# Routed tokens gathered in quarter rows and turned by VectorE instead of TensorE, in a fused MetaFormer block with a mixture of experts

## What is computed

```python
x = x + conv_ref(ln_c(x), ...)            # per channel and image a gate from mean, std, max and a median
t = to_tokens(x)                          # 2048 tokens x 512 channels
h = ln_t(t)                               # normalized tokens
logits = h @ router_w.T                   # 8 experts, the best one is taken
e, w = top_1(logits), sigmoid(top_value)
t = t + w * (silu(h @ w1[e]) * (h @ v1[e])) @ w2[e]      # routed expert
t = t + (silu(h @ sg) * (h @ su)) @ sd                   # shared expert
```

## Time and profile before

| | |
|---|---|
| three runs | 413.93 us median, 413.44 to 414.0 |
| span of the profiled execution, first to last instruction | 411.6 us |
| median less span | 2.3 us, what lies around the instructions |
| TensorE matmuls busy | 94% of the span |
| VectorE / ScalarE / GpSimd busy | 63% / 39% / 33% |

### The profile page before, as it was taken

The page is one execution under the profiler, slowest core; times in us unless marked ns, Lnnn a source line. Parts: engine busy times, 40 slices in busy tenths (PEclk is TensorE's granted clock), DMA queues, the critical chain, the costliest instruction groups (busy, mean ns, idle before and its releaser), DMA issues.

```text
span 411.6 us, 6789 instructions
## 1 busy us (share of the span) xinstructions
PE 385.1 (94%) x1982; PEld 303.8 (74%) x1986; DVE 258.2 (63%) x475; ACT 161.2 (39%) x274; POOL 134.6 (33%) x186
## 2 busy tenths in 40 slices
PE   5875659999999999999999999999999999999994
PEld 2442238888888788887888888888888888888883
DVE  6997876555857865656875557547375744676322
ACT  3996852223344324211116245153254515354110
POOL 7787811000100100005030245425535442446201
PEclk9998999999999999999999999999999999999999
DMA  8900502011201561140041469726546773752210
GB/s 321 397 2 0 204 1 78 27 51 60 90 30 53 187 247 53 53 153 27 32 133 41 128 217 323 282 98 256 204 134 219 294 258 118 262 182 71 86 37 30
DMA packets 14763, 55.96 MB, mean 136 GB/s; under 512 B 2575, under 2 KB 2575, under 8 KB 11280
## 3 DMA queue, kind: packets, MB, share of 16 engines
q1 hardware_dynamic: 9936, 40.93, 28.0%
q0 software_dynamic: 4800, 14.69, 10.0%
HBM read 43.02 MB, written 13.63 MB: 138 GB/s over the span
## 4 chain that ended last, share of the span: by engine, by line
PE 81%; DVE 7%; ACT 5%; issue 3%; POOL 2%; DMA 1%; DVEq 0%; POOLq 0%; ACTq 0%
PE GU L1255 47%; PE yb L1255 22%; PE th L1247 4%; PE tx L1240 4%; ACT tiles L534 2%; PE th L1284 2%; DVE search_junk L806 1%; ACT scratch L545 1%; ACT scratch L549 1%; DMA x_sb<-x_tok 1%; PE mb L1255 1%; DVE x_sb L864 1%; DVE tiles L862 1%; DVE bn_parts L871 1%; PE mb L1233 0%
## 5 line engine op out<-in xcount | busy, mean ns | idle before, releaser
L1255 PE MATMUL GU<-w_parts,xT 128*128 (+1 forms) x864 | 213.6, 395 | 0.0
L1255 PEld LDWEIGHTS GU<-w_parts,xT 128*128 128x128 f32 x864 | 158.3, 188 | 31.4
L1255 PE MATMUL yb<-w_parts,hT 128*128 (+1 forms) x420 | 102.6, 392 | 0.0
L1255 PEld LDWEIGHTS yb<-w_parts,hT 128*128 128x128 f32 x420 | 77.8, 188 | 15.7
L605 ACT ACTIVATE hT<-th 128x512 fp32r<-128x512 f32 x36 | 21.6, 599 | 170.8 <-PE th L1247 170.8
L472 POOL DMA_INDIRECT out<-x_sb,scatidx x20 | 37.6, 1879 | 92.5 <-DVE x_sb L1098 85.6
L922 DVE TENSOR_TENSOR w_parts<-w_raw,w_parts 128x2048 f32 (+1 forms) x24 | 54.9, 2288 | 7.4 <-issue 7.2
L907 DVE TENSOR_TENSOR hidden<-hidden,GU 128x512 f32<-128x512 f32 x36 | 24.8, 688 | 40.2 <-PE GU L1255 40.1
L522 ACT ACTIVATE w_parts<-w_raw 128x2048 f32 (+1 forms) x24 | 45.2, 1910 | 4.2 <-issue 3.9
L446 POOL TENSOR_TENSOR x_rstd<-x_mv,eps 128x1 f32<-128x1 f32 x16 | 3.0, 190 | 113.4 <-DVE x_mv L874 113.4
L901 DVE TENSOR_TENSOR hT<-th,hT 128x512 fp32r<-128x512 f32 x36 | 24.8, 689 | 23.9 <-ACT hT L605 23.6
(11 more groups left out here) (233 smaller groups left out, 339.8 us busy)
## 6 DMA issues: line engine op xcount, KB each, us to landing
w_raw<-weights SPq DMA_DIRECT2D x27, 1024.0 KB, 5.3
x_sb<-x_tok SPq DMA_DIRECT2D x8, 512.0 KB, 6.5
xn_d<-tiles SPq DMA_DIRECT2D x16, 256.0 KB, 2.0
z_d<-x_sb SPq DMA_DIRECT2D x16, 256.0 KB, 2.0
tiles<-xn_d,tokidx POOLq DMA_INDIRECT x20, 4.7
x_sb<-z_d,tokidx POOLq DMA_INDIRECT x20, 5.5
out<-x_sb,scatidx POOLq DMA_INDIRECT x20, 6.8
conv<-conv_par SPq DMA_DIRECT2D x1, 10.0 KB, 9.0
```

The costliest lines, as they stand in the source:

```text
L1255: last = pe.matmul(dst, left[:, lp, kc, :], wset(q, k, wp, kc), start=(i == 0), stop=(i == 3 * KC - 1))
```

## The change

Normalized rows are written with their channels interleaved: place 4c + f of a row holds channel 128f + c. TensorE's transposes of the shared stage read them back through the same view, with a step of four elements. A routed block is no longer gathered by one DMA of 128 rows of 512 floats, but by four DMAs of 128 rows of 128 floats (a quarter row each). The partition p of DMA j takes quarter p // 32 of the token in slot 32j + p % 32. VectorE then turns the buffer in one instruction of 32 x 32 transposes, which gives channels in the partitions (`turn_x`, into the SBUF tile `turned`, a part of `search_junk`). ScalarE and VectorE take the high and low parts from there (`turned_hi`, `turned_lo`), and TensorE's four transposes a block are gone. The indices of the quarter rows come from four small matmuls with a 0/1 matrix `dealer` (`deal_slots`) and one VectorE instruction (`quad_rows`).

```diff
+        turned = search_junk[:, 2 * P:2 * P + C]
+        dealer = turned.rearrange("p (j q r) -> p j q r", j=QUADS, q=QUADS)
...
+            xn_quads = xn_d.rearrange("t (q c) -> (t q) c", q=QUADS)
...
-                pool.indirect_dma_start(xg[:, b % RING, :], None, xn_d[:, :], rows(tokidx, b)).then_inc(xg_in[b % RING], 16)
+                for j in range(QUADS):
+                    pool.indirect_dma_start(xg[:, b % RING, j * P:(j + 1) * P], None, xn_quads, rows(quadidx[:, j, :], b)).then_inc(xg_in[b % RING], 16)
...
+            pool.wait_ge(quads_ready, 1)
             for b in range(RING):
                 gather_x(b)
...
-                pool.wait_ge(tx_done, NT + b - RING + 1)
+                pool.wait_ge(x_turned, b - RING + 1)
                 gather_x(b)
...
-                dve.tensor_scalar(tiles[:, u, :], tile_of(x_sb, t), x1_mv[:, u, 0:1], x1_rstd[:, u:u + 1], ALU.subtract, ALU.mult).then_inc(xn_ready, 1)
+                dve.tensor_scalar(interleaved(tiles[:, u, :]), tile_of(x_sb, t).rearrange("p (f c) -> p f c", f=KC),
+                                  x1_mv[:, u, 0:1], x1_rstd[:, u:u + 1], ALU.subtract, ALU.mult).then_inc(xn_ready, 1)
+
+            def turn_x(b, u, count):
+
+                dve.wait_ge(xg_in[u], count)
+                dve.wait_ge(xlo, b + NT)
+                dve.transpose(out=turned.rearrange("p (f j r) -> p f j r", f=KC, j=QUADS),
+                              in_=xg[:, u, :].rearrange("p (j c f) -> p f j c", j=QUADS, f=KC)).then_inc(x_turned, 1)
+
+            def turned_lo(n, slot):
+                dve.wait_ge(xhi, n + 1)
+                dve.wait_ge(x_turned, n - (NT - 1))
+                dve.tensor_tensor(xT[:, slot, LO, :, :], turned.rearrange("p (k t) -> p k t", k=KC),
+                                  xT[:, slot, HI, :, :].bitcast(F32), ALU.subtract).then_inc(xlo, 1)
...
+                if n == DEALER_AFTER:
+                    note(dve.tensor_copy(dealer, ident[:, :].rearrange("p (j r) -> p j r", j=QUADS).unsqueeze(2).to_broadcast([P, QUADS, QUADS, QROWS])))
...
+            def quad_rows():
+
+                dve.wait_ge(slots_dealt, 1)
+                dve.tensor_scalar(quadidx[:, :, :], tx[:, 0:QUADS * NB].rearrange("p (j b) -> p j b", j=QUADS), float(QUADS), quad[:, 0:1],
+                                  ALU.mult, ALU.add).then_inc(quads_ready, 1)
...
             def step(b, u, j, base):
+                ahead = (u + 2) % RING
+                turn_x(b + 2, ahead, j * (16 * QUADS) + 16 * QUADS * (base + 1 + (u + 2) // RING))
                 h_lo(b + NT, u % 2)
-                x_lo(b + (NT + 2), u % 2)
+                turned_lo(b + (NT + 2), u % 2)
                 gated(b + (NT + 1), 1 - u % 2)
...
-                    last = pe.transpose(tx[:, k * P:(k + 1) * P], src[:, k * P:(k + 1) * P], ident[:, :])
+                    last = pe.transpose(tx[:, k * P:(k + 1) * P], interleaved(src)[:, k, :], ident[:, :])
...
+            def deal_slots():
+
+                pe.wait_ge(slots_ready, 1)
+                for j in range(QUADS):
+                    last = pe.matmul(tx[:, j * NB:(j + 1) * NB],
+                                     turned[:, j * P:(j + 1) * P],
+                                     slotinfo[:, 0, 0:NB], start=True, stop=True)
+                last.then_inc(slots_dealt, 1)
...
-                pe.wait_ge(xg_in[ahead], j * 16 + 16 * (base + 1 + (u + 2) // RING))
-                transpose_x(n + 2, xg[:, ahead, :])
```

More of the change, by code:

```diff
@@ L24 @@
 RING = 4
+QUADS, QROWS = 4, 32
+DEALER_AFTER = 7
 SEARCH_FROM, SEARCH_TO = -24.0, 24.0
@@ L130, in program @@
         scatidx = sb("scatidx", [P, NB], U32)
+        quadidx = sb("quadidx", [P, QUADS, NB], U32)
+        quad_i = sb("quad_i", [P, 1], I32)
+        quad = sb("quad", [P, 1])
         rtmp = tiles[:, :, :].rearrange("p a c -> p (a c)")
@@ L226, in program @@
         slots_ready = sem("slots_ready")
+        slots_dealt = sem("slots_dealt")
+        quads_ready = sem("quads_ready")
+        x_turned = sem("x_turned")
         tables = sem("tables")
@@ L267, in spread_rows, with interleaved @@
             return scratch[:, of * P:to * P].rearrange("p (s b r) -> p s b r", s=to - of, b=B)
+        def interleaved(row):
+            return row.rearrange("p (c f) -> p f c", f=KC)
         def tile_of(buf, t):
@@ L595, in x_hi, with turned_hi @@
                 act.activation(xT[:, slot, HI, :, :], tx[:, :].rearrange("p (k t) -> p k t", k=KC), ACT.Copy).then_inc(xhi, 1)
+            def turned_hi(n, slot):
+                act.wait_ge(x_turned, n - (NT - 1))
+                act.activation(xT[:, slot, HI, :, :], turned.rearrange("p (k t) -> p k t", k=KC), ACT.Copy).then_inc(xhi, 1)
             def silu_gate(n, parity):
@@ L655, in _ @@
                     keep_logits(t)
-            x_hi(NT, 0)
+            turned_hi(NT, 0)
             for k in (GATE, UP):
@@ L661, in _ @@
             h_hi(NT - 1, 1)
-            x_hi(NT + 1, 1)
+            turned_hi(NT + 1, 1)
             silu_gate(NT, 0)
@@ L676, in step @@
                 h_hi(b + NT, u % 2)
-                x_hi(b + (NT + 2), u % 2)
+                turned_hi(b + (NT + 2), u % 2)
                 silu_gate(b + (NT + 1), 1 - u % 2)
@@ L713, in _ @@
             own(dve.tensor_copy(iota_f[:, :], iota_i[:, :]))
+            own(dve.tensor_scalar(quad_i[:, :], pidx_i[:, 0:1], QROWS.bit_length() - 1, None, ALU.logical_shift_right))
+            own(dve.tensor_copy(quad[:, :], quad_i[:, :]))
             own(dve.tensor_copy(pidx[:, :], pidx_i[:, :]))
@@ L1114, in _ @@
             h_lo(n + 2, 1)
+            quad_rows()
             block_experts()
@@ L1120, in _ @@
             gated(n + 4, 1)
-            x_lo(NT, 0)
+            turn_x(0, 0, 16 * QUADS)
+            turned_lo(NT, 0)
             add_shared(n + 3)
             lo_of(GATE, 1)
+            turn_x(1, 1, 16 * QUADS)
             h_lo(n + 4, 1)
-            x_lo(NT + 1, 1)
+            turned_lo(NT + 1, 1)
             gated(NT, 0)
@@ L1307, in _ @@
                 for k in (2 * half, 2 * half + 1):
-                    last = pe.transpose((th, tx)[half][:, k * P:(k + 1) * P], tiles[:, 0, k * P:(k + 1) * P], ident[:, :])
+                    last = pe.transpose((th, tx)[half][:, k * P:(k + 1) * P], interleaved(tiles[:, 0, :])[:, k, :], ident[:, :])
                 last.then_inc(tx_half if half == 0 else tx_done, 1)
@@ L1375, in _ @@
             transpose_h(n + 2, 1)
+            deal_slots()
             up_product(n + 3, 2, 0, 0, 0)
@@ L1380, in _ @@
             up_product(n + 4, 3, 1, 0, 0)
-            pe.wait_ge(xg_in[0], 16)
-            transpose_x(NT, xg[:, 0, :])
             down_product(n + 3, 0, 0, 0)
@@ L1385, in _ @@
             transpose_h(n + 4, 1)
-            pe.wait_ge(xg_in[1], 16)
-            transpose_x(NT + 1, xg[:, 1, :])
             up_product(NT, 0, 0, 1, 3)
@@ L1392, in step @@
                 n = b + NT
-                ahead = (u + 2) % RING
                 at, after = table_entries(pe, b, range(SET_COL, SET2_COL + 1))
```

## The result

The changed kernel takes 417.66 us in the median of four runs (417.46 to 417.95), the one before 413.9 us beside it (413.44 to 414.0). The ratio is 1.0094, 95% interval 1.0079 to 1.0108: slower by 3.8 us, where +1.9 was forecast. Differences of 0.2% can be told apart here, so the sign is certain.

A forecast was written before the change was run, and what follows sets the result against it. The prediction took TensorE as the bound, busy for all of the routed window. Its terms, -8.8 transposes, +1.1 dealing, +0.3 normalizing and +9.3 late gathers, made +1.9 us: 415.8 us, range 406.2 to 420.5.

The forecast's parts named there:

- strided transposes: Shared stage, TensorE reading with a step of four: taken as no cost, bounds nothing to 5.8 us.
- cover of VectorE's list: Routed steps behind gate-up steps: 0.1 us of slack left before h_lo; if gone, 2.5 us of stalls.
- rival D: Routed stage: VectorE becomes the bound, 18 turns adding 12 us; no chance of its own, price of 2.5 us in C.
- Transposes removed: Twenty routed blocks lose four TensorE transposes each: 8.8 us gained, a step falling from 9.09 to 8.65 us.
- Dealing: Before the routed stage, four index matmuls and a wait for tokidx on TensorE's path: 1.1 us lost, matmuls 0.6.
- Normalizing and the shared transposes: Shared stage: norm_tile's interleaved write delays the first tile, 0.3 us lost; the strided reads add nothing.
- The turn: Routed stage, VectorE's transposing instruction ahead of h_lo: 0.68 us each, bounds 0.55 to 1.22, barely covered.
- GpSimd's list: Routed stage: quarter gathers held by weight splits deliver x late, 145 us for 15 blocks, TensorE stalls 9.3 us; chance 0.55.
- the signs named: Profile rows expected if right: GpSimd nearly never idle, gathers of 2 to 3 us, turns awaiting x, down products awaiting h_lo.
- C: Rival: the 16-byte step costs double everywhere, 2.9 us in transposes, 2.5 behind gate-up steps; alone 411.9 us, chance 0.08.
- The net of the routed stage: Routed stage: gain of the removed transposes against stalls from late gathers, -8.8 and +9.3 us, forecast +0.5.
- C with A: Rival: doubled cost of the 16-byte step together with GpSimd being late, 418.7 us, chance 0.10.

The follow-up runs named there:

- runs: Changed kernel with no step of 16 bytes: tiles hold runs of 32 neighbouring channels, gate, up and router matrix rows laid out to match; 414.94 us, ratio 1.0027.
- no_hold_short: Changed kernel, routed weight splits read a PSUM bank in place of the high part, and the turn moves only 128 of 512 elements; 410.34 us, ratio 0.9911.
- one_gather: Changed kernel with each block of x gathered by one DMA instead of four, the turn kept; 416.1 us, ratio 1.0056.
- one_gather_short: Changed kernel with one gather DMA a block and a turn of only 128 of 512 elements; 411.14 us, ratio 0.9925.
- turn_late: Changed kernel with VectorE's turn placed behind h_lo, same work; 418.15 us, ratio 1.0110.
- no_hold: Changed kernel, the routed loop's weight splits read a PSUM bank in place of the high part in SBUF; 415.56 us, ratio 1.0032.
- short_turn: Changed kernel with the turn moving only 128 of 512 elements of a partition, all else kept; 416.73 us, ratio 1.0061.
- mixed2: As runs, but only two blocks in four quartered and turned, others gathered whole and transposed by TensorE, dealing behind the up product; 412.96 us, ratio 0.9972.
- turn_plain: Changed kernel with the turn reading runs of 32 neighbouring elements instead of every fourth one; 416.9 us, ratio 1.0071.
- turn_psum: Changed kernel with the turn writing to a PSUM bank instead of SBUF, both parts taken from there; 420.98 us, ratio 1.0172.
- no_deal: Changed kernel without the dealing matmuls, quad_rows taking indices from slotinfo; 419.45 us, ratio 1.0134.

## Why the prediction was right and wrong

The measured loss is twice the forecast one. For the number, the step that failed is the sum's term for the shared stage, above all the strided transposes, put at nothing; the 0.3 us that it had for both were 1.15 us. For the mechanism, it is the length of the turn and with it the cover of VectorE's list: rival D, taken for nothing by itself, is one of the two causes.

**Transposes removed, -8.8 us.** Right: 8.64 us a step.

**Dealing, 1.1 us.** 1.42 us. The four fp32 matmuls run as eight and take 0.91 us, the upper bound, where I took 0.6.

**Normalizing and the shared transposes, 0.3 us together.** The step that failed first. `norm_tile` took 0.744 us, inside its bounds, but the transposes, at "I take nothing, as no row shows an engine slowed by a layout", cost 0.035 us a tile (a row of four takes 0.39 us, before 0.355), 0.56 us in all, and a tile normalized late held TensorE for 0.39 us at 143.69. With 0.2 us at the first tile that makes 1.15 us, the 1.2 us between runs and no_hold_short. The rest of the 1.85 us is the fall of the clock (0.47) and the late first `norm_tile` (0.38), less the 0.14 us by which the execution was ahead; the prediction had no term for either. "No row shows it" was an argument for the middle of the bounds, not for their lower end.

**The turn, 0.68 us.** Mis-sized: 1.09 us, of which 0.39 is the step of 16 bytes. My two ends were 0.55 and 1.22 us, and I called the cover 0.1 us wide. With the turn at 1.09 it is gone. Rival D got no chance of its own and a price of 2.5 us. With GpSimd's list short, a turn of 1.09 us in place of 0.40 costs 5.0 us (one_gather less one_gather_short). That it is so much fits turn_late's rows, where the turn also heads the chain over ScalarE's high parts to the next split, which the slack of one step doesn't show.

**GpSimd's list, +9.3 us.** The length was right: 144.9 us for 145. Nineteen DMAs in that stretch were held by splits and lost 29.7 us (28 reckoned), three by `turned_lo` and lost 0.8 (2.6 reckoned). The hold is shown, and stalls of 8.4 us came for the 9.3 forecast. But they weren't the stalls I described: taken away alone the holds give 2.1 us (no_hold), and 6.4 us once the turn is short (short_turn to no_hold_short). "Unhindered, the turn of x(19) would have to start at 382.5" held for a TensorE that nothing else delays, and VectorE delayed it. The turn of x(19) did start at 392.55, for the 392 forecast, and the down product behind it started at 395.10 without an idle row: by then TensorE was as late as GpSimd. That the two times agree is in part luck: the list started at 240.9, not 237.7, and the landing was 2.7 us in the median, not the 5.7 I took:

```profile
DMA to landing us min/median/max: 2.4/2.7/6.9
```

So of the signs named, GpSimd without idle time, gathers of 2 to 3 us and waits of down products for `h_lo` came; so did a turn over 1 us, a sign of C, while the pitch of the shared transposes was 0.39/4 = 0.098 us, under its 0.11. The turns waited for x three times only, 3.7 us.

**The sum.** Between the two profiled executions 1.55 us too little are ahead of `fill_slots` and 0.3 the dealing; of the 1.55, 0.85 are the layout. The net of the routed stage, +0.6 us for +0.5, came out right although the stalls had another cause in part: that is luck. C with A, priced at 418.7, was nearest to 417.66, and its price was not right either: the layout costs the shared stage 1.15 us, not 2.9.

## What to carry to other kernels

When two engines each run close to the pace of the one that bounds, price them together: taking one away shows only what the other doesn't hide, 0.9 and 1.6 us here, where both are worth 6.5. Moving work off the bounding engine pays up to the point where the receivers' lists are full, and a mix (every second block) beat moving it all: mixed2 is 2.0 us faster than runs, of which the new place of the dealing (0.96 us for 1.42) gives 0.5. An access with a step of 16 bytes is a cost to write into the sum: 0.2 us on a pass of 0.55, 0.39 us on one of 0.70, 65 ns on a weight load of 140.

## What the runs showed of the chip

- A VectorE operation with two SBUF inputs (2.29 us) held a GpSimd indirect DMA until it ended, and one with an input in PSUM didn't: mean 1.23 and 0.95 us for the same DMA.
- TensorE's clock fell from 2.4 to 1.2 GHz right behind five stalls of 2.36 to 3.04 us, one in each of short_turn, turn_plain, runs, turn_psum and no_deal, and not behind the one of 1.94 us in short_turn. The length of the stall doesn't settle it: after a wait of 1.82 us ahead of the first tile (62.5 to 62.7) the granted clock was 0.50 from 64 to 66 us in no_hold and 1.00 in no_hold_short. In runs 0.56 was granted from 356 to 358 us, and the down product took 4.46 us in place of 2.72. Such a late gather costs its wait and, in these five, 1.45 to 1.74 us more in the down product.

```profile
355.50 4.62 PE L1309 MATMUL yb<-w_parts,hT 128*128 x12 [2.65 <-DVE hT L942]
359.96 2.23 PE L1309 MATMUL GU<-w_parts,xT 128*128 x9
```

```profile
356.00:358.00 2.00, 2.00 (x7) 1.55 (x6) 0.69 (x2) 1.79 (x1) 1.41 (x2) 0.56 0.90 334
```

- A quarter gather landed in 2.7 us in the median, a whole one in 4.7; issuing, not moving, is what quarters cost.
- 32 x 32 transposes of 128 x 512 fp32 on VectorE take 0.70 us from runs of 32.
